# Output projection of an attention block: one 256-column matmul for both batches of a pair, in two slots of a chunk instead of four

## What is computed

```python
k, q, v = split_heads(ctx @ Wk.T + bk), split_heads(layernorm(x) @ Wq.T + bq), split_heads(ctx @ Wv.T + bv)
score = einsum('bhij,bhkj->bhik', k, q) / sqrt(8)        # 16 heads of 8
attn  = softmax(score, axis=1)                            # over the 16 heads
out   = einsum('bhik,bhij->bhjk', attn, v)                # then reshaped to [batch, 128, 64] and transposed
x     = x + out @ Wo.T + bo
x     = x + ffn(layernorm(x))                             # 3 blocks: linear, layernorm, gelu, linear, + residual
```

## The kernel before

| slot | before the projection | projection (L836) | L938 | after it |
|---|---|---|---|---|
| 0 | L890: ctx transposes | quarter 1 of c-2 | yes | L948: x transposes |
| 1 | L894: q, 512 columns | quarter 2 of c-2 | yes | L955: needs the q eviction |
| 2 | L898: k, 512 columns | quarter 3 of c-2, then `s_wo` | yes | L959: needs the k eviction |
| 3 | L830, L907: v; L830: bias rows into `wo_ps` | quarter 0 of c-1 | yes | |

## Time and profile before

### The profile page before, as it was taken

How to read it: one execution, slowest core, us unless ns; L and a number is a source line. 1 busy time by engine, 2 the same in 40 slices (tenths; PEclk the granted TensorE clock), 3 DMA queues, 4 the chain that set the end, 5 groups by cost and what they waited for, 6 DMA issues and landing times.

```text
span 405.0 us, 11901 instructions
## 1 busy us (share of the span) xinstructions
PE 366.2 (90%) x4205; PEld 258.1 (64%) x4205; DVE 351.3 (87%) x863; ACT 290.1 (72%) x542; POOL 288.0 (71%) x349
## 2 busy tenths in 40 slices
PE   2778999999999999999989777788999999999964
PEld 1334566677667766776656556566877887787631
DVE  4746999999999999999999999878999999888852
ACT  3447887888788878787766534358888888888741
POOL 5681998789878987898797878757667766744320
PEclk9999999999999999999999989999999999999995
DMA  5636765476547654675444100000000010001011
GB/s 164 181 105 210 218 199 150 141 235 186 159 133 221 203 159 136 201 213 163 144 133 147 39 2 2 1 2 2 28 28 26 26 52 26 28 27 53 27 53 52
DMA packets 53120, 43.26 MB, mean 107 GB/s; under 512 B 4496, under 2 KB 46944, under 8 KB 53088
## 3 DMA queue, kind: packets, MB, share of 16 engines
q1 hardware_dynamic: 53088, 42.84, 35.2%
HBM read 26.05 MB, written 16.78 MB: 106 GB/s over the span
## 4 chain that ended last, share of the span: by engine, by line
PE 67%; DVE 15%; POOL 7%; issue 6%; ACT 3%; DMA 1%; POOLq 0%; ACTq 0%; DVEq 0%
PE score_ps L973 8%; PE att_ps L938 7%; PE score_ps L869 7%; PE score_ps L878 6%; PE wo_ps L836 6%; PE work L1020 4%; DVE negmax L529 3%; DVE zsum L550 3%; PE score_ps L1020 3%; PE work L894 3%; PE att_ps L1020 3%; PE work L907 2%; PE score_ps L966 2%; PE score_ps L830 2%; PE work L898 2%
## 5 line engine op out<-in xcount | busy, mean ns | idle before, releaser
L373 POOL TENSOR_TENSOR probs<-probs,rz 128x1024 f32<-128x1024 f32 x64 | 136.4, 2141 | 34.0 <-DVE rz L553 33.6
L409 POOL TENSOR_TENSOR rs<-ve,minus_half 128x8 f32<-128x8 f32 (+1 forms) x40 | 55.6, 1390 | 53.4 <-DVE ve L516 53.4
L529 DVE TENSOR_REDUCE negmax<-score_ps 128x64 bf16<-128x1024 f32 x64 | 76.1, 1189 | 7.7 <-PE score_ps L869 7.6
L659 ACT ACTIVATE probs<-score_ps 128x1024 f32<-128x1024 f32 x64 | 65.6, 1025 | 23.5 <-PE score_ps L878 23.1
L550 DVE TENSOR_REDUCE zsum<-probs 128x64 f32<-128x1024 f32 x64 | 77.5, 1211 | 5.6 <-ACT probs L659 5.0
L751 ACT ACTIVATE z<-score_ps,nmr,rs 128x128 f32<-128x128 f32 x160 | 60.4, 469 | 15.3 <-POOL nmr L412 15.1
L836 PEld LDWEIGHTS wo_ps<-wo_t,att_t 128*128 128x128 f32 x256 | 37.5, 193 | 13.8 <-issue 12.2
L938 PE MATMUL att_ps<-probs,v_diag 128*32 128x64 f32 x2048 | 43.9, 225 | 1.4 <-POOL probs L373 1.4
L878 PE MATMUL score_ps<-negmax,ident_bf 128*128 128x512 bf16 x128 | 39.2, 388 | 5.6 <-DVE negmax L529 5.5
L973 PEld LDWEIGHTS score_ps<-lin_t,h 128*128 128x128 f32 x320 | 42.1, 192 | 1.3
L973 PE MATMUL score_ps<-lin_t,h 128*128 128x128 f32 x320 | 42.1, 275 | 0.0
(11 more groups left out here) (152 smaller groups left out, 727.6 us busy)
## 6 DMA issues: line engine op xcount, KB each, us to landing
q_parts<-parts SPq DMA_DIRECT2D x16, 512.0 KB, 3.6
q_stack<-q_parts SPq DMA_DIRECT2D x64, 128.0 KB, 2.8
k_stack<-k_parts SPq DMA_DIRECT2D x32, 256.0 KB, 3.3
ctx_sb<-in_ctx SPq DMA_DIRECT2D x16, 256.0 KB, 3.7
k_parts<-parts SPq DMA_DIRECT2D x16, 256.0 KB, 2.7
out<-x_all SPq DMA_DIRECT2D x16, 256.0 KB, 2.3
x_all<-in_x SPq DMA_DIRECT2D x14, 256.0 KB, 3.9
x_all<-in_x SPq DMA_DIRECT2D x1, 512.0 KB, 5.0
```

The costliest lines, as they stand in the source:

```text
L373: nc.gpsimd.tensor_tensor(e[:, :, :, :], e[:, :, :, :], by_query.broadcast_to([P, BANDS, SEQ, ADJ]), ALU.mult).then_inc(s_probs, 1)
L409: nc.gpsimd.tensor_tensor(rs2[b][:, lo:hi], ve2[b][:, lo:hi], minus_half[:, lo:hi], ALU.pow).then_inc(p_rs[b], 1)
L529: nc.vector.tensor_reduce(negmax[p % 2][:, :], score_ps[p % 2][:, :].rearrange("p (h k) -> p k h", k=SEQ), AX_X, ALU.max, negate=True).the ...
L659: nc.scalar.activation(probs[p][:, :, :, :], score_ps[p % 2][:, :].rearrange("p (u s k) -> p u k s", s=ADJ, k=SEQ), ACT.Exp, scale=SCALE). ...
```

## The change

`project_out` now takes u alone. Its two matmuls (o = 0, 1) have both batches of `wo_t` as moving operand, 256 columns, and write half of `wo_ps`. Half 0 is computed in slot 3 of chunk c from chunk c-1's `att_t`, where quarter 0 was; half 1 in slot 1 of the next chunk, where quarter 2 was. Slots 0 and 2 have no projection; `s_wo` is signalled in slot 1 instead of 2. Both halves are as before sums over the same products.

```diff
-            def project_out(t, att):
-
-                b, u = t % 2, t // 2
+            def project_out(u, att):
+
                 for o in range(2):
-                    ins = nc.tensor.matmul(wo_ps[:, TILE * t:TILE * (t + 1)], att[:, o, TILE * u:TILE * (u + 1)],
-                                           wo_t[:, o, b, :], start=False, stop=o == 1, skip_group_check=True)
+                    ins = nc.tensor.matmul(wo_ps[:, 2 * TILE * u:2 * TILE * (u + 1)], att[:, o, TILE * u:TILE * (u + 1)],
+                                           wo_t[:, o, :, :], start=False, stop=o == 1, skip_group_check=True)
                 return ins
...
                         project_out(0, att_t[1 - par])
-                    if p < 3 and live(c - 2):
-                        ins = project_out(p + 1, att_t[par])
-                        if p == 2:
-                            ins.then_inc(s_wo, 1)
+                    if p == 1 and live(c - 2):
+                        project_out(1, att_t[par]).then_inc(s_wo, 1)
```

## The result

| | before | with the change |
|---|---|---|
| median | 407.35 us (9 runs, 405.55 to 407.8) | 409.31 us (9 runs, 408.31 to 410.52) |
| profiled execution, span | 406.81 us, 405.0 us | 410.29 us, 408.5 us |

The ratio is 1.0067 with a 95% interval of 1.0045 to 1.0089: slower by 0.7%, where 410.8 us, 0.8% slower, was forecast. The spans of the two profiled executions differ by 3.5 us.

A forecast was written before the change was run, and what follows sets the result against it. TensorE was taken to bound the loop, VectorE close behind. Slots of -0.445, +0.415, -0.08 and +0.415 make +0.305 us a chunk, +3.3 us in all: 410.8 us against the median, range 409.2 to 412.6.

The forecast's parts named there:

- The bound: Loop from 60 to 200 us: belongs to TensorE, with VectorE close behind; what follows belongs to VectorE until attention ends.
- Slot 0: Loop chunk, slot 0: loses a projection quarter, -0.445 us; nothing ahead of the next L878 is late there.
- Slot 1: Loop chunk, slot 1: four 256-column records at 215 ns, 0.86 us for 0.445, +0.415; L955 does not wait.
- rival 3: Projection matmuls: width is cheap, a 256-column record under 177 ns makes it faster, 403.1 us at 111 ns; chance 0.08.
- Slot 2: Loop chunk, slot 2: loses a quarter, but TensorE waits some 0.36 us for k eviction L716, so only -0.08 us.
- rival 2: Slot 2: the stall does not come, ScalarE's eviction follows TensorE's earlier arrival; no change, 407.1 us; chance 0.08.
- Slot 3: Loop chunk, slot 3: +0.415 us; VectorE's equal lateness is absorbed by its 0.44 us idle in slot 2 and the longer slot.
- The sum: Whole program: +0.305 us a chunk, +3.05 over ten chunks, +0.415 in chunk 1, -0.15 elsewhere; +3.3 us.
- Rival 1: Later chunks: one more VectorE instruction caught behind GpSimd, as L507 in step 0; +1.8 us, 412.6 us; chance 0.06.
- theory A: From the experiments: projection in slots 1 and 2 covers ScalarE's evictions; its place alone costs, not its width.

The follow-up runs named there:

- the control: Kernel before the change, with only the subtraction of k's high part moved from slot 2 to behind slot 3's scores; ratio 0.9978 to before.
- the version with all three moves in the four slots: Against the kernel before: one 256-column matmul per slot, q's and k's subtractions behind the next slot's scores, x transposes earlier in slot 0; ratio 1.0009.
- the version with both subtractions later: Against the kernel before: one 256-column matmul in each of four slots, q's and k's high-part subtractions moved behind the next slot's scores; ratio 1.0007.

## Why the prediction was right

- **The bound.** TensorE bounds the loop and the order of its waits decides: the runs without a quarter show 0.44 us in slot 0 and 0.08 in slot 2 for the same work.
- **Slot 0**, -0.445: measured 3.17 to 2.73, -0.44.
- **Slot 1**, +0.415 from a record of 215 ns that the trace of before did not have: in the changed kernel L835 takes 105.94 - 104.98 = 0.96 us, four records of 215 ns and 0.10 for the switch. Measured +0.42. The line through 128 and 512 columns held, and rival 3 with it failed: at half of that pitch the time would have fallen.
- **Slot 2**, -0.08: measured 3.34 to 3.25. The eviction ended 0.06 us ahead of L956, as in chunk 1. That chunk's slot, outside the hardware loop, was the evidence against rival 2, and its 2.30 us was not the loop's value: 109.80 - 107.42 = 2.38.
- **Slot 3**, +0.415: measured 3.49 to 3.91. VectorE was late for the scores by 0.3 us a chunk, as said. But its idle time in slot 2 did not absorb any of this: the wait for L659 is 4.4 us in ten chunks as before. The longer chunk alone made room for it.
- **The sum.** +0.305 a chunk against +0.32; ten chunks +3.2 for +3.05; chunk 1 +0.40 for +0.415; at the first matmul after the wait in chunk 13, 211.63 for 208.08, 3.55 us later, and at the end of the span 3.5. That these two agree is partly luck: behind chunk 13, chunk 14 is 0.33 us longer than before and chunk 15 is 0.41 shorter, where the forecast had nothing in chunk 14 and -0.03 at chunk 15's end. The profiled execution came out at 410.29 us for 410.1. The median, 409.31, is 1.5 us under the 410.8 forecast, and the difference of the medians, 2.0 us, is under the 2.7 us of the ratio: the nine executions of the kernel before fall into two groups 2 us apart (405.55 to 405.94 and 407.35 to 407.8), with the median in the upper one, and a median of nine can jump between such groups. The forecast's 3.3 us lies inside the ratio's interval, 1.8 to 3.6 us.
- **Rival 1** did not occur as priced: in step 0 L507 took 1.95 us, where it had taken 1.97, and ended at 209.80 with GpSimd's multiplications (209.78), so both moved together. The next long ones are nearly the same in both kernels (0.88, 1.48, 1.48 and 0.95 us for 0.88, 1.49, 1.47 and 0.60), and the part behind the attention is no longer than before (158.1 us for 158.2).
- **Not foreseen**: the 0.10 us of a switch was seen in slot 2 and called a cost "whatever stands ahead"; that moving a matmul past the scores would save one was found only by the control. And that theory A would allow any place with both evictions covered was too simple, as the run with halves in slots 1 and 2 showed.

## What to carry to other kernels

Work on the bounding engine that stands between the start and the use of another engine's result is worth only its slack if taken out, and its full price where it is put in: here -0.08 and +0.42 us for the same 0.44. Before merging or moving matmuls, look in each slot for the eviction that is used next and for the distance from its end to its use; a distance near the shortest one in the trace (0.06 us here) means no room. And look for a stretch of the old trace that already runs without the piece, such as a first chunk: it shows the wait that the edit will uncover.

## What the runs showed of the hardware

**A switch from full width to narrow tiles costs about 0.10 us.** Told above: from the projection to L938 it was 0.54 us for four records of 111 ns, and one switch less gave 0.11 us a chunk. It isn't the same in every place: the switch saved by q's later subtraction gave 0.08 us in slot 1 (3.32 to 3.24), of which slot 3 lost 0.04 again, and the one saved in slot 0 gave 0.16 us where `v_diag` was ready (2.73 to 2.57) and nothing where it was not. That the width of the tiles is the cause was not tested apart from the place of the matmul.

**The clock at the end of the program moves a time by 1.9 us.** The last stage by stretch (us, busy us and instructions of each engine, granted clock, DMA), first the kernel before and then the version without slot 2's quarter:

```profile
395.00:400.00 5.00, 3.19 (x6) 1.22 (x6) 1.00 (x2) 1.29 (x3) 0.00 (x0) 0.50 0.16 52
```

```profile
395.00:400.00 5.00, 1.78 (x6) 0.71 (x6) 1.44 (x2) 0.28 (x1) 0.00 (x0) 1.00 0.17 54
```

Six matmul records, four of 128 columns and two of 512 in both stretches, take 3.19 us at 1.2 GHz and 1.78 at 2.4. In both, TensorE is partly idle before that; in one trace the clock falls ahead of the last matmuls, in the other behind. From the last L878 to the end it is 158.1 us in the first trace and 155.8 in the second, and 1.9 of these 2.3 us arise in the last three groups of matmuls, which take 1.11, 2.07 and 1.11 us at 1.2 GHz and 0.65, 1.13 and 0.66 at 2.4. The clock isn't all of the spread: the version with all three moves in the four slots has its last matmuls at 2.4 GHz and takes 157.8 us all the same. What lengthens the earlier part was not found.

**A wait in chunk 12 is followed by a slot at half the clock in some traces.** At the end of chunk 12 TensorE waits for the maximum behind VectorE's first feed-forward statistics, and longer where it gets there sooner. In the version with halves in slots 1 and 2:

```profile
209.88 0.88 PE L877 MATMUL score_ps<-negmax,ident_bf 128*128 128x512 bf16 x2 [1.85 <-DVE negmax L529]
...
210.55 1.06 PE L889 MATMUL work<-ident,ctx_sb 128*128 128x128 f32 x4
```

Four records that take 0.60 us elsewhere take 1.06: the clock was granted at 1.2 GHz for this slot, which lasted 4.25 us instead of 2.7. The version without slot 0's quarter shows the same there (L878 with 2.07 us of idle time ahead, L890 at 1.06, slot 4.14 us), and so does the four-slot version with the x transposes early (2.41 us of idle time, slot 4.58 us). In the kernel before, with 1.77 us of idle time, the clock stayed up and the matmul is the last of the earlier trace rows. But the length of the wait does not decide it. In the version with both subtractions later, the clock stayed up behind the longest wait at this place:

```profile
206.18 0.60 PE L886 MATMUL score_ps<-negmax,ident_bf 128*128 128x512 bf16 x2 [2.46 <-DVE negmax L529]
```

The change with k's subtraction later kept it, too, behind 1.97 us. What decides was not found, and with one trace for each kernel it isn't shown that the edits cause it: the 1.4 us that such a slot costs are a risk of this wait in any of them.
